# A mixture of experts on one core: tokens gathered in quarter rows and turned by VectorE instead of TensorE

## The chip, the cores and the metric

The program runs on one core of a Trainium2 chip. The metric is the device time of one execution in microseconds (us), the median over runs. PE is TensorE, DVE is VectorE, ACT is ScalarE, POOL is GpSimd; SP only issues loads and stores.

## What is computed

Two batches of 2048 tokens of 512 numbers go through cross attention, a quantised feed-forward layer, a mixing layer, and then a feed-forward layer of 16 experts. Each stage works on the layer norm of its input and adds its result to it. Only the last stage matters here:

```
logits = x @ Wg + bg                       # [2, 2048, 16]
probs  = softmax over the tokens           # each expert weighs all tokens
vals, idx = top_k(probs of one expert, 128)
tok = x[batch, idx]                        # 2 x 16 x 128 tokens of 512
h   = relu(tok @ w1[e] + b1[e])
h   = relu(h @ w2[e] + b2[e])
out = (h @ w3[e] + b3[e]) * vals
y   = zeros.at[batch, idx].add(out)
```

## The kernel before, in words

The first three stages run tile by tile (32 tiles of 128 tokens) and write the normed input of the last stage, xn4, to memory, one row of 2 KB for each token, besides the running result `out`. Then the tokens of each expert are chosen, and the experts follow. For the first four experts of batch 0 this is done early ("early experts", `early_tokens`). The rest are the twelve "joint" experts 4 to 15 for both batches (256 tokens each; e counts them from 0 to 11), and the first four experts of batch 1 alone ("single", s from 0 to 3, 128 tokens each), which are put into the joint experts e = 1, 4, 7 and 9 (`SINGLE`).

A product of a joint expert is made in three passes: each operand is split into a rounded part ("hi", made by ACT) and the rest ("lo", made by DVE: `lo`, L1973), for weights (1 MB each; `split_hi`, `split_lo`) as for tokens (`token_hi`, `token_lo`). A layer of a joint expert (`hidden`) is 48 matmuls, its last product (`outputs`) 24. Singles multiply in plain fp32.

The order on each engine is written out by hand, and each engine works through its list in order:

- PE, for each e: [`single_tokens`], `hidden(e, 0)`, [`single_first`], `tokens(e+1)`, `outputs(e-1)`, [`single_second`], `hidden(e, 1)`, [`single_outputs`]; what stands in brackets only where a single belongs to e. `tokens` turns the gathered rows of the next expert with eight transposes of 128 by 128 into PSUM, `single_tokens` those of a single with four; the products need the features on the partitions.
- DVE, for each e: `split_lo`, two `hidden_lo`, `token_lo(e+1)` out of PSUM, then twice `split_lo` and `weighted(e-1, n)`, then two `hidden_lo`.
- ACT the same in the hi parts; it also copies the turned tokens of a single (`single_copy`).
- POOL issues the indirect DMAs: `gather(e)` fetches the 128 token rows of each batch (two DMAs of 128 rows of 2 KB), `gather_single(s)` one more, `add(e)` and `add_single(s)` add results to rows of `out`. At the start of the joint experts its order is: `gather(0)`, `gather(1)`, `gather_single(0)`, `add_early(3)`, then for each e `gather(e+2)`, [`gather_single(s+1)`, `add_single(s)`,] `add(e-1)`.
- SP loads raw weights three ahead; `load_raw(i)` waits until the lo part of weight i - 3 is made.

The list of the chosen tokens comes as rows of numbers, is turned by PE and written to `ids` by DVE (semaphore k_pos = 1); the weights `vals` follow (k_pos = 2). PE runs idle products (`keep_warm`) up to the first tokens.

Of the kernel before, what the change touches and what calls it, by code (L numbers as in the profile page):

```python
# [48 lines left out]
def build(nc, io):  # L49
# [36 lines left out]
        p_ev a_ev p_sv a_sv s_gather  # L86
# [32 lines left out]
    segbase = place("segbase", [P, 1])  # L119
    bq = place("bq", [P, C])  # L120
# [167 lines left out]
    assert top[0] <= at_xt1, (top[0], at_xt1)  # L288
    tok_s = place("single_tok", [P, D], at=at_lists)
# [5 lines left out]
    tok_h, tok_l = place("tokT_h", [P, C, B * P], F32R), place("tokT_l", [P, C, B * P], F32R)  # L295
    tokT_s, h1_s = place("single_tokT", [P, D]), place("single_h1", [P, D])
# [61 lines left out]
    def four_transposes(pe, bank, src):  # L358

        for c in range(C):  # L360
            last = pe.transpose(bank[:, c * P:(c + 1) * P], src[:, c * P:(c + 1) * P], ident[:, :])  # L361
        return last

# [200 lines left out]

    def used(eng, i):
# [11 lines left out]
    def _(sp):  # L577
# [45 lines left out]
        sp.dma_start(segbase[:, :], io.segbase).then_inc(sm.c_late, 16)  # L623
        for dst, src in ((b1, io.b1), (b2, io.b2), (b3, io.b3)):
            sp.dma_start(dst[:, :], rows_on_all(src, E)).then_inc(sm.c_late, 16)
        def load_early(i):

            layer, e = ((0, 0), (0, 1), (1, 0), (1, 1), (2, 0), (2, 1),
                        (0, 2), (0, 3), (1, 2), (1, 3), (2, 2), (2, 3))[i]
            sp.dma_start(w_e[RING[i % 5]][:, :, :], chunked(io.w[layer][e])).then_inc(sem_early[i % 5], 16)  # L630
# [57 lines left out]
        def load_raw(i):  # L688
            e, layer = order[i]
            if i >= RAW:  # L690
                sp.wait_ge(sm.a_w, i - RAW + 1)
                lo_done(sp, i - RAW)
            sp.dma_start(w_raw[i % RAW][:, :, :], chunked(io.w[layer][FIRST + e])).then_inc(sem_raw[i % RAW], 16)

        def load_single(s, layer):

            i = 3 * s + layer
            if i < 4:
                sp.wait_ge(sm.p_ev, EV["y3"])
            else:  # L700
                at, was = divmod(i - 4, 3)
                sp.wait_ge(sm.p_sv, 4 * at + was + 2)
            sp.dma_start(w_e[i % 4][:, :, :], chunked(io.w[layer][s])).then_inc(sem_early[i % 4], 16)
# [39 lines left out]
    def _(pe):  # L743
# [240 lines left out]
        def early_tokens(e):  # L984

            bank = early_bank(EV[f"t{e}"] - 1)
            pe.wait_ge(sem_tok_e[e], 16)
            four_transposes(pe, bank, tok_e[e]).then_inc(sm.p_ev, 1)
# [313 lines left out]
        keep_warm(2, warm, ps_y[0])  # L1302
# [4 lines left out]
        def tokens(e):  # L1307
            for b in range(B):
                pe.wait_ge(sem_tok[e % 2][b], 16 * (e // 2 + 1))
                if e == 0:  # L1310
                    pe.wait_ge(sm.k_pos, 2)
                else:
                    pe.wait_ge(sm.d_tlo, B * (e - 1) + b + 2)
                    if b == 1 and e - 1 in SINGLE:
                        pe.wait_ge(sm.a_sv, 4 * SINGLE[e - 1] + 1)
                for c in range(C):
                    bank = token_bank(e, b, c)
                    last = pe.transpose(bank[:, c * P:(c + 1) * P], tok[e % 2][:, b, c * P:(c + 1) * P], ident[:, :])  # L1318
                last.then_inc(sm.p_tok, 1)

        def hidden(e, layer):
# [3 lines left out]
            if layer == 0:  # L1325
                pe.wait_ge(sm.d_tlo, 2 if e == 0 else B * (e + 1) + 1)
# [4 lines left out]
            for pair in range(2):  # L1331
# [3 lines left out]
                if layer == 1 and e in SINGLE:  # L1335
                    pe.wait_ge(sm.a_sv, 4 * SINGLE[e] + 2 + pair)
# [40 lines left out]
        def outputs(e):  # L1377
# [3 lines left out]
            for b in range(B):  # L1381
# [3 lines left out]
                if b == 1 and e in SINGLE:  # L1385
                    pe.wait_ge(sm.a_sv, 4 * SINGLE[e] + 4)
# [10 lines left out]
        def single_tokens(s, u):  # L1397

            pe.wait_ge(sm.s_gather, 16 * (s + 1))
            pe.wait_ge(sm.d_tlo, B * u + 3)  # L1400
            four_transposes(pe, ps_tok[1], tok_s).then_inc(sm.p_sv, 1)

        def single_first(s, u):
# [3 lines left out]
            pe.wait_ge(sm.a_sv, 4 * s + 1)  # L1407
            early_layer(ps_hid[2], w, tokT_s, range(C)).then_inc(sm.p_sv, 1)

        def single_second(s, u):  # L1410
# [3 lines left out]
            pe.wait_ge(sm.a_sv, 4 * s + 2)  # L1414
            early_layer(ps_hid[3], w, h1_s, range(C)).then_inc(sm.p_sv, 1)

        def single_outputs(s, u):
# [3 lines left out]
            pe.wait_ge(sm.a_sv, 4 * s + 3)  # L1421
# [40 lines left out]
        tokens(0)  # L1462
        keep_warm(3, wh, ps_y[0])
        for e in range(JOINT):
            if e in SINGLE:
                single_tokens(SINGLE[e], e)
# [3 lines left out]
            if e + 1 < JOINT:  # L1470
                tokens(e + 1)
# [14 lines left out]
    def _(act):  # L1486
# [413 lines left out]
        def single_copy(s):  # L1900

            act.wait_ge(sm.p_sv, 4 * s + 1)
            act.activation(tokT_s[:, :], ps_tok[1][:, :], ACT.Copy).then_inc(sm.a_sv, 1)

        def single_relu(s, layer):

            act.wait_ge(sm.p_sv, 4 * s + 2 + layer)
# [3 lines left out]
        def single_weighted(s, u):  # L1911

            act.wait_ge(sm.p_sv, 4 * s + 4)
# [6 lines left out]
        token_hi(0)  # L1920
        nxt = AHEAD
        for e in range(JOINT):
# [3 lines left out]
            if e in SINGLE:  # L1926
                single_copy(SINGLE[e])
# [6 lines left out]
            if e + 1 < JOINT:  # L1934
                token_hi(e + 1)
# [16 lines left out]
    def _(dve):  # L1952
# [571 lines left out]
        dve.tensor_scalar(top_v[:, :], ge[1][0:HEADS, :], gmax[:, 3:4], None, ALU.mult).then_inc(sm.k_out, 1)  # L2524
        dve.wait_ge(sm.k_tr, 2)
# [8 lines left out]
        def token_lo(e):  # L2534
            for b in range(B):
                t = slice(b * P, (b + 1) * P)
                for i, part in enumerate(token_parts(e, b)):
                    dve.wait_ge(sm.a_thi, B * e + b + 1 + (i if e == 0 else 1))
                    lo(sm.d_tlo, tok_l[:, part, t], in4(token_bank(e, b, part.start))[:, part, :], tok_h[:, part, t])
# [18 lines left out]
        token_lo(0)  # L2558
        split_lo(1)
        nxt = 2  # L2560
        for e in range(JOINT):
# [5 lines left out]
            if e + 1 < JOINT:  # L2567
                token_lo(e + 1)
            for n in range(2):
# [3 lines left out]
                if e >= 1:  # L2573
                    weighted(e - 1, n)
            hidden_lo(e, 1, 0)
# [12 lines left out]
    def _(pool):  # L2588
# [219 lines left out]
        def gather_single(s):  # L2808

            if s >= 1:  # L2810
                pool.wait_ge(sm.p_sv, 4 * s - 3)
            r = E + s
            pool.indirect_dma_start(
                out=tok_s[:, :], out_offset=None, in_=io.xn4,
                in_offset=bass.IndirectOffsetOnAxis(ap=ids[:, r:r + 1], axis=0),
            ).then_inc(sm.s_gather, 16)

        def add_single(s, u):

            r = E + s  # L2820
            pool.wait_ge(sm.a_sv, 4 * s + 4)
# [5 lines left out]

        def gather(e):
            if e >= 2:
                pool.wait_ge(sm.p_tok, B * (e - 1))  # L2830
            for b in range(B):
                r = b * E + FIRST + e
                pool.indirect_dma_start(
                    out=tok[e % 2][:, b, :], out_offset=None, in_=io.xn4,
                    in_offset=bass.IndirectOffsetOnAxis(ap=ids[:, r:r + 1], axis=0),
                ).then_inc(sem_tok[e % 2][b], 16)
# [19 lines left out]
        gather(0)  # L2856
# [44 lines left out]
LATE = 16 * 7  # L2901
# [36 lines left out]
```

## Time and profile before

| | |
|---|---|
| median of 3 runs | 745.3 us (744.64 to 745.97) |
| span of the profiled execution | 743.2 us, from the first to the last instruction |
| its own device time | not listed apart from the span; the median of the runs is 2.1 us above the span |
| PE busy | 716.2 us, 96% of the span |
| DVE, ACT, POOL busy | 521.6, 401.9 and 420.4 us |
| mean granted clock of PE | 0.991 |

The joint experts fill the time from 475 to 735 us of the span. A timeline's line gives the start, the duration, the engine, the line of the kernel, the operation with what it writes and reads, and in brackets how long the engine had been idle and who released it. The clock is a share of full speed, 1.00 for 2.4 GHz and 0.50 for 1.2 GHz.

### The profile page before, as it was taken

The numbers are of one execution on the slowest core, as the hardware profiler recorded it, in microseconds if no ns is written. First come the engines' busy times: TensorE is split into PE (matmuls) and PEld (weight loads), VectorE is DVE, ScalarE is ACT, GpSimd is POOL, SyncE is SP. The second block draws the span as 40 slices with busy tenths as digits, with TensorE's granted clock in tenths as the row PEclk, the third lists the DMA queues.
The fourth block names the chain that finished last, engine by engine and source line by source line (L and its number), as shares of the span: only waits on it lengthen the run. The fifth ranks groups of instructions, "written<-read, shape, count | busy, mean of one in ns | idle before, by whom it ended". The sixth has DMA issues, their size and how long they took to land.

```text
span 743.2 us, 12766 instructions
## 1 busy us (share of the span) xinstructions
PE 716.2 (96%) x4513; PEld 624.9 (84%) x4513; DVE 521.6 (70%) x978; ACT 401.9 (54%) x680; POOL 420.4 (57%) x621
## 2 busy tenths in 40 slices
PE   6999999999999999999999799999999999999994
PEld 5765888888888888888888778798999899899894
DVE  5786789889888888876896697464663565463561
ACT  5755444444544545868668334364664656464641
POOL 2825788888888887786788622503521443340132
PEclk9999999999999999999999899999999999999998
DMA  9610121221222213111117898696796698895534
GB/s 317 256 30 15 43 86 62 88 86 58 88 79 82 71 58 108 52 60 44 49 45 264 322 396 279 149 391 186 222 370 185 185 330 293 289 266 167 142 86 58
DMA packets 61671, 118.04 MB, mean 159 GB/s; under 512 B 6056, under 2 KB 7464, under 8 KB 61608
## 3 DMA queue, kind: packets, MB, share of 16 engines
q1 hardware_dynamic: 54312, 100.44, 38.7%
q0 software_dynamic: 7296, 16.78, 10.3%
q8 instruction: 37, 0.61, 0.3%
q14 instruction: 26, 0.21, 0.1%
HBM read 91.76 MB, written 25.21 MB: 157 GB/s over the span
## 4 chain that ended last, share of the span: by engine, by line
PE 84%; issue 6%; DMA 4%; DVE 3%; ACT 2%; POOL 1%; POOLq 0%; SPq 0%; DVEq 0%; ACTq 0%
PE bank L354 39%; PE banks L354 9%; PE bank L361 6%; PE bank L994 6%; PE banks L861 4%; PE banks L867 4%; DMA out<-y,ids 3%; PE banks L871 2%; PE banks L994 2%; PE banks L872 2%; PE banks L1423 1%; PE banks L1028 1%; PE bank L1318 1%; PE bank L1041 1%; DMA out<-x 1%
## 5 line engine op out<-in xcount | busy, mean ns | idle before, releaser
L2844 POOL DMA_INDIRECT out<-y,ids x24 | 46.1, 1922 | 157.4 <-DVE y L2555 155.5
L1973 DVE TENSOR_TENSOR w_l<-w_raw,w_h 128x2048 fp32r<-128x2048 f32 x35 | 80.1, 2291 | 63.2 <-ACT w_h L1496 49.4
L1961 DVE BATCH_NORM_STATS2 bn<-x 128x6 f32<-128x512 f32 x113 | 77.7, 688 | 8.2 <-DMA x<-x 5.4
L1496 ACT ACTIVATE w_h<-w_raw 128x2048 fp32r<-128x2048 f32 x36 | 68.5, 1918 | 7.2 <-DMA w_raw<-w 7.2
L1892 ACT ACTIVATE h<-bank,b 128x512 f32<-128x512 f32 x48 | 33.0, 688 | 62.5 <-PE bank L354 57.8
L1973 DVE TENSOR_TENSOR hT_l<-h,hT_h 128x512 fp32r<-128x512 f32 x48 | 33.0, 689 | 39.8 <-ACT hT_h L1898 37.7
L354 PE MATMUL bank<-tokT_h,w_h 128*128 128x256 f32 x188 | 55.1, 293 | 0.0
L2607 POOL TENSOR_SCALAR rstd<-mean_var 128x1 f32<-128x1 f32 x108 | 25.7, 238 | 50.9 <-DVE mean_var L1966 42.6
L354 PE MATMUL bank<-tokT_h,w_l 128*128 128x256 f32 x188 | 53.2, 283 | 0.0
L354 PE MATMUL bank<-tokT_l,w_h 128*128 128x256 f32 x188 | 53.2, 283 | 0.0
L354 PE MATMUL bank<-wf_h,xdT_h 128*128 128x512 f32 x128 | 52.6, 411 | 0.0
L354 PE MATMUL bank<-wf_h,xdT_l 128*128 128x512 f32 x128 | 50.3, 393 | 0.0
L354 PE MATMUL bank<-hT_h,w_h 128*128 128x256 f32 x176 | 50.1, 285 | 0.0
L354 PE MATMUL bank<-wf_l,xdT_h 128*128 128x512 f32 x128 | 50.0, 390 | 0.0
L354 PE MATMUL bank<-hT_l,w_h 128*128 128x256 f32 x176 | 49.8, 283 | 0.0
L354 PE MATMUL bank<-hT_h,w_l 128*128 128x256 f32 x176 | 49.8, 283 | 0.0
L1650 ACT ACTIVATE q<-bank,bq 128x512 f32<-128x512 f32 x32 | 22.0, 688 | 45.0 <-PE bank L354 44.5
L2687 POOL TENSOR_TENSOR x<-x,mix_bias 128x512 f32<-128x512 f32 x32 | 41.3, 1292 | 1.9 <-PE bank L361 1.8
L2625 POOL TENSOR_TENSOR qT_l<-q,qT_h 128x512 fp32r<-128x512 f32 x32 | 41.4, 1295 | 0.7 <-ACT qT_h L1652 0.7
L2723 POOL TENSOR_TENSOR x<-x,ffn_bias 128x512 f32<-128x512 f32 x32 | 41.8, 1305 | 0.0
L1492 ACT ACTIVATE xn<-x,rstd 128x512 f32<-128x512 f32 x32 | 26.1, 816 | 24.4 <-POOL rstd L2622 20.8
L1973 DVE TENSOR_TENSOR xdT_l<-bank,xdT_h 128x512 fp32r<-128x512 f32 x32 | 22.0, 689 | 23.7 <-ACT xdT_h L1496 23.4
(419 smaller groups left out, 2380.1 us busy)
## 6 DMA issues: line engine op xcount, KB each, us to landing
w_raw<-w SPq DMA_DIRECT2D x36, 1024.0 KB
early_w<-w SPq DMA_DIRECT2D x24, 1024.0 KB, 10.0
x<-x SPq DMA_DIRECT2D x32, 256.0 KB, 2.7
out<-x SPq DMA_DIRECT2D x32, 256.0 KB, 2.0
xn<-xn SPq DMA_DIRECT2D x32, 256.0 KB
mask<-mask_t SPq DMA_DIRECT2D x8, 256.0 KB, 3.4
slot_all<-slots SPq DMA_DIRECT2D x4, 512.0 KB, 7.8
stage<-wk SPq DMA_DIRECT2D x1, 1024.0 KB, 7.7
```

The lines of the kernel that those rows point to most:

```text
L354: last = pe.matmul(out, a, b, start=(n == 0), stop=(n == 3 * len(pairs) - 1))
L361: last = pe.transpose(bank[:, c * P:(c + 1) * P], src[:, c * P:(c + 1) * P], ident[:, :])
L861: last = pe.matmul(both_halves[:, a, 0:WIDE], xh[:, d, :], wc_h[:, d, a, :], start=(d == 0), stop=(d == C - 1))
L994: last = pe.matmul(bank[:, c * P:(c + 1) * P], w[:, d, c * P:(c + 1) * P], x[:, d * P:(d + 1) * P], start=(d == 0), stop=(d == C - 1))
L1496: act.activation(dst, src, ACT.Copy).then_inc(sem, 1)
L1892: act.activation(h32[n % 2][:, :], ps_hid[n % 4][:, :], ACT.Relu, bias=bias)
L1961: dve.bn_stats(bn6[which][:, j % 2, :], src[:, :]).then_inc(sem_bn[which], 1)
L1973: dve.tensor_tensor(dst, src, hi_part, ALU.subtract).then_inc(sem, 1)
L2625: pool.tensor_tensor(dst, src, hi_part, ALU.subtract).then_inc(sem, 1)
L2687: pool.tensor_tensor(x2[j % 2][:, :], x2[j % 2][:, :], cbias[:, batch(j), :], ALU.add).then_inc(sm.g_x2b, 1)
L2723: pool.tensor_tensor(x1_of(k)[:, :], x1_of(k)[:, :], fbias[:, :], ALU.add).then_inc(sm.g_x1b, 1)
L2844: pool.indirect_dma_start(out=out_rows, out_offset=bass.IndirectOffsetOnAxis(ap=ids[:, r:r + 1], axis=0), in_=y[e % 2][b][:, :], in_offset ...
```

## The change

The tokens of all joint experts but the first, and of the singles, are no longer gathered as whole rows. The row of 512 numbers is taken as four quarters of 128. One indirect DMA now fetches, for 32 tokens, the four quarters of each onto four groups of 32 partitions, so a set of 128 tokens takes four DMAs of 128 pieces of 512 bytes instead of one of 128 pieces of 2 KB. DVE then turns the 32 by 32 blocks of the result (`turn_blocks`, one instruction for 128 tokens), which puts feature 4p + c on partition p. ACT and DVE make the hi and lo parts out of that SBUF copy, for both batches in one instruction each, instead of out of PSUM in two. `tokens` and `single_tokens` leave PE, and `single_copy` leaves ACT. The first joint expert and the early experts are gathered and turned as before, but PE reads their rows with a step of four, and the weights of the first layers are loaded with four rows for each partition in one piece of 8 KB. The numbers of the quarter rows (`quarter_ids`) are made once: ACT repeats the chosen numbers times four, PE turns them with four transposes, and DVE adds the number of the quarter.

```diff
+    quarter_ids = place("quarter_ids", [P, C, ROWS], U32, at=at_seg)
+    tok_raw = place("tokT_raw", [P, C, B * P], at=at_qt + 4 * KB)
+    def of_chunk(rows, c):
+        return rows[:, c::C]
+    def turn_blocks(eng, out, rows):
+        return eng.transpose(out.rearrange("p c (t k) -> p t c k", k=QBLK),
+                             rows.rearrange("p (t k c) -> p t c k", t=P // QBLK, c=C))
+    def expert_weights(layer, e):
+        w = io.w[layer][e]
+        return w.rearrange("(p c) n -> p c n", c=C) if layer == 0 else chunked(w)
@@ @block.tensor, end of the choice @@
-        keep_warm(2, warm, ps_y[0])
+        pe.wait_ge(sm.a_rep, 1)
+        for t in range(C):
+            last = pe.transpose(ps[5][:, 2 * t * ROWS:2 * t * ROWS + HEADS], exps[0:HEADS, t * P:(t + 1) * P],
+                                ident[0:HEADS, 0:HEADS])
+        last.then_inc(sm.k_tq, 1)
@@ @block.tensor, joint experts @@
-        tokens(0)
+        first_tokens()
         for e in range(JOINT):
-            if e in SINGLE:
-                single_tokens(SINGLE[e], e)
             hidden(e, 0)
             if e in SINGLE:
                 single_first(SINGLE[e], e)
-            if e + 1 < JOINT:
-                tokens(e + 1)
@@ @block.scalar @@
+        act.wait_ge(sm.k_ids, 1)
+        act.activation(exps[0:HEADS, :].rearrange("p (t q k) -> p t q k", t=C, k=QBLK),
+                       top_i[:, :].rearrange("p (t k) -> p t k", k=QBLK).unsqueeze(2)
+                       .to_broadcast([HEADS, C, P // QBLK, QBLK]), ACT.Copy, scale=float(P // QBLK)).then_inc(sm.a_rep, 1)
...
         def token_hi(e):
-            for b in range(B):
-                act.wait_ge(sm.p_tok, B * e + b + 1)
-                act.wait_ge(sm.p_h, max(0, 4 * (e - 1) + 2))
-                for part in token_parts(e, b):
-                    hi(sm.a_thi, tok_h[:, part, b * P:(b + 1) * P], in4(token_bank(e, b, part.start))[:, part, :])
+            act.wait_ge(sm.d_tr, B * e)
+            hi(sm.a_thi, tok_h[:, :, :], tok_raw[:, :, :])
...
             for n in range(2):
                 if nxt < len(order) and (e > 0 or n == 1):
                     split_hi(nxt)
                     nxt += 1
+                if n == 0 and e + 1 < JOINT:
+                    token_hi(e + 1)
@@ @block.vector @@
+        dve.wait_ge(sm.k_tq, 1)
+        dve.tensor_scalar(quarter_ids[:, :, :],
+                          ps[5][:, 0:2 * C * ROWS].rearrange("p (t r) -> p t r", t=C)[:, :, 0:HEADS:2],
+                          quarter[:, 0:1], None, ALU.add).then_inc(sm.k_quart, 1)
         dve.wait_ge(sm.k_tr, 2)
         dve.tensor_copy(vals[:, :], ps[0][:, 0:HEADS:2]).then_inc(sm.k_pos, 1)
...
+        def turn_tokens(e):
+            dve.wait_ge(sm.p_h, 4 * e - 2)
+            for b in range(B):
+                dve.wait_ge(sem_tok[e % 2][b], tokens_in(e))
+                turn_blocks(dve, tok_raw[:, :, b * P:(b + 1) * P], tok[e % 2][:, b, :]).then_inc(sm.d_tr, 1)
+        def token_lo(e):
+            dve.wait_ge(sm.a_thi, e + 3)
+            lo(sm.d_tlo, tok_l[:, :, :], tok_raw[:, :, :], tok_h[:, :, :])
+        def turn_single(s):
+            dve.wait_ge(sm.s_gather, 64 * (s + 1))
+            if s >= 1:
+                dve.wait_ge(sm.p_sv, 3 * s - 2)
+            turn_blocks(dve, tokT_s[:, :].rearrange("p (c t) -> p c t", c=C), tok_s[:, :]).then_inc(sm.d_ts, 1)
...
             hidden_lo(e, 0, 0)
             hidden_lo(e, 0, 1)
             if e + 1 < JOINT:
-                token_lo(e + 1)
+                turn_tokens(e + 1)
+            if e + 1 in SINGLE:
+                turn_single(SINGLE[e + 1])
             for n in range(2):
                 if nxt < len(order):
                     split_lo(nxt)
                     nxt += 1
                 if e >= 1:
                     weighted(e - 1, n)
+                if n == 0 and e + 1 < JOINT:
+                    token_lo(e + 1)
@@ @block.gpsimd @@
+        xn4_quarters = io.xn4.rearrange("n (q f) -> (n q) f", q=P // QBLK)
         def gather(e):
-            if e >= 2:
-                pool.wait_ge(sm.p_tok, B * (e - 1))
+            if e == 2:
+                pool.wait_ge(sm.p_tok, B)
+            if e >= 3:
+                pool.wait_ge(sm.d_tr, B * (e - 2))
             for b in range(B):
                 r = b * E + FIRST + e
-                pool.indirect_dma_start(
-                    out=tok[e % 2][:, b, :], out_offset=None, in_=io.xn4,
-                    in_offset=bass.IndirectOffsetOnAxis(ap=ids[:, r:r + 1], axis=0),
-                ).then_inc(sem_tok[e % 2][b], 16)
+                for t in range(C):
+                    pool.indirect_dma_start(
+                        out=tok[e % 2][:, b, t * P:(t + 1) * P], out_offset=None, in_=xn4_quarters,
+                        in_offset=bass.IndirectOffsetOnAxis(ap=quarter_ids[:, t, r:r + 1], axis=0),
+                    ).then_inc(sem_tok[e % 2][b], 16)
...
         pool.wait_ge(sm.k_pos, 1)
-        gather(0)
+        first_gather()
+        pool.wait_ge(sm.k_quart, 1)
         gather(1)
         gather_single(0)
         add_early(3)
```

## Rows read from the trace of the kernel before

**Rows 1.** Busy time by engine, joint experts (us, busy (instructions) PE PEld DVE ACT POOL, clock, DMA share, GB/s).

```profile
475.00:735.00 260.00, 258.75 (x1844) 239.22 (x1844) 142.71 (x131) 140.85 (x167) 82.15 (x53) 1.00 0.76 231
```

**Rows 2.** The chain that ended last, in order of time (start us, us, what).

```profile
487.75 0.44 PE bank L361 x4
488.19 5.76 PE bank L354 x48
493.95 3.57 PE bank L994 x32
497.52 0.87 PE bank L1318 x8
498.40 5.47 PE banks L354 x24
...
646.28 5.75 PE bank L354 x48
...
664.55 5.76 PE bank L354 x48
```

**Rows 3.** GpSimd's timeline (start us, us, line, operation, idle before and releaser).

```profile
468.60 1.03 POOL L2833 DMA_INDIRECT tok<-xn,ids  x1 [3.62 <-DMA out<-early_tok,early_ids]
469.93 0.98 POOL L2833 DMA_INDIRECT tok<-xn,ids  x1 [0.30 <-issue]
471.22 0.95 POOL L2833 DMA_INDIRECT tok<-xn,ids  x1 [0.31 <-issue]
472.47 0.94 POOL L2833 DMA_INDIRECT tok<-xn,ids  x1 [0.30 <-issue]
...
556.26 2.52 POOL L2833 DMA_INDIRECT tok<-xn,ids  x1 [0.30 <-issue]
...
642.78 1.76 POOL L2844 DMA_INDIRECT out<-y,ids  x1 [7.33 <-DVE y L2555]
644.85 1.02 POOL L2833 DMA_INDIRECT tok<-xn,ids  x1 [0.30 <-issue]
```

**Rows 4.** GpSimd's timeline at the early experts: last logit gather, its first reader.

```profile
426.24 0.94 POOL L2778 DMA_INDIRECT early_logit<-cut,early_logit_ids  x1 [0.30 <-issue]
432.35 0.20 POOL L2789 TENSOR_TENSOR early_shift<-early_logit,cut_tops 128x4 f32<-128x4 f32 x1 [5.17 <-DMA early_logit<-cut,early_logit_ids]
```

**Rows 5.** TensorE's timeline: after the long wait; first reader of the second gather.

```profile
417.79 1.11 PE L915 MATMUL bank<-ident,lg_wide 128*128 128x128 f32 x4 [4.95 <-DVE lg_wide L2124]
...
473.44 0.44 PE L1318 MATMUL bank<-ident,tok 128*128 128x128 f32 x2 [0.27 <-issue]
```

**Rows 6.** VectorE's timeline.

```profile
475.22 2.28 DVE L1973 TENSOR_TENSOR w_l<-w_raw,w_h 128x2048 fp32r<-128x2048 f32 x1
...
482.44 0.69 DVE L1973 TENSOR_TENSOR hT_l<-h,hT_h 128x512 fp32r<-128x512 f32 x1 [2.13 <-ACT hT_h L1898]
...
555.64 2.29 DVE L1973 TENSOR_TENSOR w_l<-w_raw,w_h 128x2048 fp32r<-128x2048 f32 x1 [1.11 <-ACT w_h L1496]
...
641.70 0.81 DVE L2555 TENSOR_SCALAR y<-banks,b,vals 128x512 f32<-128x512 f32 x1
```

**Rows 7.** Busy time by engine in short stretches (columns as in rows 1).

```profile
416.00:418.00 2.00, 0.21 (x1) 0.22 (x2) 1.49 (x7) 2.00 (x3) 1.24 (x4) 0.51 0.75 290
422.00:423.00 1.00, 1.00 (x7) 1.00 (x7) 1.00 (x5) 0.00 (x0) 0.55 (x1) 0.57 0.99 377
424.00:430.00 6.00, 6.00 (x56) 6.00 (x56) 5.90 (x16) 1.27 (x3) 2.57 (x3) 1.00 1.04 398
486.00:490.00 4.00, 4.00 (x36) 4.00 (x35) 3.93 (x4) 3.16 (x5) 0.00 (x0) 1.00 1.03 401
655.00:660.00 5.00, 5.00 (x31) 4.42 (x30) 4.11 (x4) 2.91 (x2) 0.56 (x1) 1.00 0.99 296
```

**Rows 8.** ScalarE's timeline: the last exponential of the token choice.

```profile
466.89 0.40 ACT L1876 ACTIVATE ge<-top_v,gmax 63x128 f32<-63x128 f32 x1 [0.33 <-DVE gmax L2510]
```

**Rows 9.** The load queue's timeline: three 1 MB loads.

```profile
478.02 4.25 SPq L703 DMA_DIRECT2D early_w<-w  x3
```

More of the change, by code:

```diff
@@ L119, in build @@
     segbase = place("segbase", [P, 1])
+    quarter = place("quarter", [P, 1])
     bq = place("bq", [P, C])
@@ L362, in four_transposes, with four_row_transposes @@
         return last
+    def of_chunk(rows, c):
+        return rows[:, c::C]
+    def four_row_transposes(pe, bank, rows):
+        for c in range(C):
+            last = pe.transpose(bank[:, c * P:(c + 1) * P], of_chunk(rows, c), ident[:, :])
+        return last
+    def turn_blocks(eng, out, rows):
[4 more added lines that the diff above has]
+        return w.rearrange("(p c) n -> p c n", c=C) if layer == 0 else chunked(w)
     def blocks(t):
@@ L563, in token_bank, with tokens_in @@
         return ps_y[1] if (e, b) == (0, 1) and c >= 2 else ps_tok[b]
+    def tokens_in(e):
+        return 64 * (e // 2) + (16 if e % 2 == 0 else 64)
     def used(eng, i):
@@ L623, in _ @@
         sp.dma_start(segbase[:, :], io.segbase).then_inc(sm.c_late, 16)
+        sp.dma_start(quarter[:, :], io.quarter).then_inc(sm.c_late, 16)
         for dst, src in ((b1, io.b1), (b2, io.b2), (b3, io.b3)):
@@ L1301, in _, with first_tokens @@
         pe.transpose(ps[1][:, 0:HEADS], top_i[:, :], ident[0:HEADS, 0:HEADS]).then_inc(sm.k_tr, 1)
-        keep_warm(2, warm, ps_y[0])
+        pe.wait_ge(sm.a_rep, 1)
[3 more added lines that the diff above has]
+        last.then_inc(sm.k_tq, 1)
         pe.wait_ge(sm.k_out, 1)
         pe.transpose(ps[0][:, 0:HEADS], top_v[:, :], ident[0:HEADS, 0:HEADS]).then_inc(sm.k_tr, 1)
-        def tokens(e):
+        def first_tokens():
             for b in range(B):
[L1309 to L1315, printed above, removed]
+                pe.wait_ge(sem_tok[0][b], 16)
+                pe.wait_ge(sm.k_pos, 2)
                 for c in range(C):
-                    bank = token_bank(e, b, c)
-                    last = pe.transpose(bank[:, c * P:(c + 1) * P], tok[e % 2][:, b, c * P:(c + 1) * P], ident[:, :])
+                    bank = token_bank(0, b, c)
+                    last = pe.transpose(bank[:, c * P:(c + 1) * P], of_chunk(tok[0][:, b, :], c), ident[:, :])
                 last.then_inc(sm.p_tok, 1)
@@ L1325, in hidden @@
             if layer == 0:
-                pe.wait_ge(sm.d_tlo, 2 if e == 0 else B * (e + 1) + 1)
+                pe.wait_ge(sm.d_tlo, 2 if e == 0 else e + 3)
                 xh, xl = tok_h, tok_l
@@ L2532, in split_lo, with first_token_lo @@
             lo(sm.d_w, w_l[i % WR][:, :, :], w_raw[i % RAW][:, :, :], w_h[i % WR][:, :, :])
-        def token_lo(e):
+        def first_token_lo():
             for b in range(B):
                 t = slice(b * P, (b + 1) * P)
-                for i, part in enumerate(token_parts(e, b)):
-                    dve.wait_ge(sm.a_thi, B * e + b + 1 + (i if e == 0 else 1))
-                    lo(sm.d_tlo, tok_l[:, part, t], in4(token_bank(e, b, part.start))[:, part, :], tok_h[:, part, t])
+                for i, part in enumerate(token_parts(0, b)):
+                    dve.wait_ge(sm.a_thi, b + 1 + i)
+                    lo(sm.d_tlo, tok_l[:, part, t], in4(token_bank(0, b, part.start))[:, part, :], tok_h[:, part, t])
+        def turn_tokens(e):
+            dve.wait_ge(sm.p_h, 4 * e - 2)
+            for b in range(B):
+                dve.wait_ge(sem_tok[e % 2][b], tokens_in(e))
[8 more added lines that the diff above has]
+            turn_blocks(dve, tokT_s[:, :].rearrange("p (c t) -> p c t", c=C), tok_s[:, :]).then_inc(sm.d_ts, 1)
         def hidden_lo(e, layer, pair):
@@ L2556, in weighted @@
                               ALU.add, ALU.mult).then_inc(sm.d_y, 1)
-        token_lo(0)
+        first_token_lo()
         split_lo(1)
@@ L2925 @@
     arrays["later"] = -(p[:, None] > p[None, :]).astype(np.float32)
+    arrays["quarter"] = (p // 32).astype(np.float32).reshape(P, 1)
     arrays["segbase"] = (p // 64 * 2048 + p % 4 * 512).astype(np.float32).reshape(P, 1)
```

65 lines of the change are left out of this document (33 added, 32 removed).

## The prediction

> **What bounds the kernel now.** I read the busy time of the joint experts first. Of 260 us between 475 and 735, PE is busy 258.75 at full clock, DVE 142.71, ACT 140.85, POOL 82.15 [rows 1]. The reader is to see that this stage ends when PE ends, and that whatever leaves PE's list is a gain as long as nothing on PE begins to wait. The chain of waits in order of time says the same piece by piece: a layer of 48 matmuls takes 5.75 us, an output of 24 takes 5.47, a single's layer 3.57, the eight transposes of an expert 0.87, the four of a single 0.44, one behind the other without a gap [rows 2]. Then POOL's timeline, because gathers are multiplied by four there; DVE's, which gets a new place to wait; the short stretches for the clock and the DMA share.
>
> **What leaves PE.** Eleven expert turns of 0.87 and four single turns of 0.44: 9.57 + 1.76 = 11.33 us [rows 2]. This is all that can be won here. ACT's single copies and the PSUM reads of ACT and DVE are off the path (both are idle over 40% of the stage [rows 1]).
>
> **What POOL gets.** Gathers follow each other every 1.25 us (471.22, then 472.47), of which 0.94 to 1.03 is the DMA instruction itself [rows 3]. Does a gather of 64 KB cost less to issue than one of 256 KB? The logit gathers fetch 128 pieces of 4 bytes and take 0.94 us [rows 4], so the price goes with the 128 indices, not the bytes. I take 1.25 each. Gathers grow by 6 for each of 11 experts and by 3 for each of 4 singles: 78 more, 97.5 us; POOL's 82 of 260 become 180. That fits on average. It doesn't fit where a gather has no lead, and there are two such places, both singles, because `turn_single` now waits on DVE one expert earlier, in front of the `split_lo` and `token_lo` that the next first layer on PE needs.
>
> **First place: expert 1.** Its single 0 is gathered twelfth after `gather(0)`. The first quarter gather starts at 471.22, where `gather(1)` starts now [rows 3]; the new list isn't later (ACT's copy of 63x512, between 0.40 for 63x128 and DVE's 0.69 for 128x512, four small transposes and one DVE operation come after ACT's last exponential, over at 467.29, and shortly before `gather(0)` at 468.60; they are done near 470 [rows 3, 6, 8]). The twelfth starts at 471.22 + 11 x 1.25 = 484.97 and ends at 485.9. One hit comes on top: a gather that starts while DVE subtracts weights (2.29 us) is held to about 0.85 us past that operation's end (started 556.26, lasted 2.52 instead of 0.98; DVE's began at 555.64 [rows 3, 6]). DVE subtracts from 475.22 to 477.50, so some 1.2 us: 487.1.
>
> Landing: `gather(0)`'s second DMA left POOL at 470.91 and PE reads it at 473.44, 2.5 us at most [rows 3, 5]. The last logit gather left at 427.18 and its reader came at 432.35, 5.2 us, with the DMA engines full (share 1.04) [rows 4, 7]. At 486 to 490 the share is 1.03 now [rows 7], but the next load hangs on the delayed `split_lo`, so the three megabytes issued from 478.02 on [rows 9] will be nearly through; I take 4.0 and keep 2.5 and 5.2. So 491.1. The Trainium skill, "DMA: Bandwidth & Descriptors", section "Anatomy of one DMA — SWDGE (gpsimd) path", gives some 2.0 us plus bytes over 436 GB/s, an estimate of 2.15 us here; by it the two places together would cost 3.7 us less, and the logit row speaks against it where the engines are full.
>
> Then on DVE: the turn, `split_lo` 2.29, `token_lo` for 128x1024 at half of that, 1.15, handovers 0.2. No DVE turn is in the trace. The nearest row is a subtraction of 128x512 out of SBUF, 0.69 us [rows 6], which I take; the upper bound is a 128x2048 operation, 2.29 (each number at four times the price), the lower 0.6. The Trainium skill, "SBUF — State Buffer", section "Door 1: The DMA port swizzle", in its note on 16-byte lines, says that an access that goes to a new line each time pays a penalty; the turn reads with a step of four numbers, 16 bytes. No row here shows such a step, so the sum stays with 0.69; by the page it would move to the upper bound, some 3 us more in all.
>
> 491.1 + 0.69 + 2.29 + 1.15 + 0.2 = 495.4, where PE starts this layer at 487.95 now (488.19 in the chain, which models ends [rows 2]): 7.5 later. The bounds are 492.6 (+4.7: no hit, landing 2.5) and 499.4 (+11.5: two hits, 5.2, slow turn). PE is done with expert 0 at about 487.6 and idles for some 8 us; its eight transposes there covered a handover, so their removal brings nothing forward.
>
> The clock: after 4.95 us of idling [rows 5] PE ran at a granted 0.50, the 1.2 GHz level, from about 417.8 until 422.9 [rows 7]; 5.1 us at half speed lose 2.5. I add 2.5 here (bounds 0 and 2.5): 10.0 in all.
>
> What else queues there is covered: `add_early(3)`, behind the twelve gathers, lets `relu(0,1,0)` go near 493 instead of 485, and `gather(2)` lands near 506, but expert 1 holds a single, and its 27 us on PE (two layers, an output and three single products of some 3.6) give DVE and ACT the time.
>
> **Second place: expert 9.** Count from T, the start of expert 8's first layer, 646.28 now [rows 2]. `gather(10)` follows the second `add(6)`, whose y DVE ends at 642.51; that is tied to PE by the single of expert 7 and stays. So it starts no earlier than T - 1.4 [rows 3], and single 3 comes behind its eight DMAs: the twelfth ends at T - 1.4 + 11 x 1.25 + 0.95 = T + 13.3. One hit, 1.2, and POOL's own lag: between `gather(2)` at 489 and this point lie 84 gathers and 16 adds (105 + 28 us) and up to 21 hits (25 us) in some 158 us, so POOL is about full and 0 to 4 us behind; I take 1.5. T + 16.0, landed T + 20.0; turn 0.69, `split_lo` 2.29, `weighted` 0.81 [rows 6], `token_lo` 1.15, 0.2: T + 25.2. PE starts expert 9 at T + 18.3 now [rows 2]: 6.9 later, and 2.5 of clock (it idles from T + 17.0), 9.4. Bounds: T + 20.8, that is +2.5 without the clock, and T + 29.4, +11.1 with it 13.6.
>
> **Where nothing waits.** Singles 1 and 2 are gathered one round of POOL earlier; by the same count single 1 lands some 2 us before its turn, single 2 hardly before, with 1 us left at expert 7. Expert turns have a round of lead. In an expert without a single `token_lo` ends some 3.5 us before PE needs it, which covers two turns even at 2 us. `quarter_ids` puts k_pos = 2 back by 0.5, of which 0.2 shows, as PE waits for the gather anyway. The strided PE reads of six token sets are bounded by nothing and doubling (6 x 0.4, not all on the path); I take 0. The 8 KB weight pieces gain nothing, since no PE wait is put down to a load.
>
> **Sum.** Transposes not eaten by the two places: 11.33 - 2 x (0.87 + 0.44) = 8.7 won. 10.0 + 9.4 + 0.2 - 8.7 = 10.9 us longer: span 754, and as the median stands 2.1 above the span, 756 us. All lower bounds: 4.7 + 2.5 - 8.7 = -1.5, 744. All upper: 14.0 + 13.6 + 0.2 - 8.7 and up to 2 of strided reads, 766.
>
> **Rivals.**
> 1. It is hidden: the singles land before DVE wants them, and only the transposes go. 11.33 less about 0.8 of the handover they covered: 735. It decides from a last single gather landed by 483.6 (487.95 - 4.35), so issue below (483.6 - 2.5 - 471.2) / 12 = 0.83 us each. For it: POOL is idle for two thirds of the stage [rows 1]. Against it: 1.25 us apart, and 0.94 for 4-byte pieces [rows 3, 4].
> 2. The waits come at their lowest price, the gathers landing in 2.5 us without a hit, and idling of 4 to 5 us leaves the clock alone: 744, even or a hair faster. For it: the loads are held back too, so the DMA engines may be free. Against it: the one row with 4.95 us idle lost the clock.
> 3. POOL becomes the bound: hits pile up, it falls over 4 us behind, expert 7 waits too, adds come late: 766. For it: 133 us of issue in 158. Against it: during each DVE wait no weight is subtracted, so there are no hits.
>
> **Chances.** Forecast 0.62 (its own range 748 to 763), rival 1 0.07, rival 2 0.15, rival 3 0.16. The predicted time is 756. For 8 in 10 the range must reach into rivals 2 and 3: 744 to 766. A change below 0.2% is about what a measurement of this kernel can't tell from none. Faster: rival 1 and a part of 2, 0.13; same: most of the rest of 2, 0.10; slower 0.77.
>
> **What the new profile would show.** Quarter gathers 1.25 us apart, twelve of them after 471; POOL busy near 180 us in the stage; DVE turns near 0.7 us; PE idle before the first layers of experts 1 and 9, released by DVE's `token_lo` (L1973), with the clock at 0.5 behind both; no gap elsewhere above 1 us; transposes gone from the chain. I'd be wrong if quarter gathers were issued in under 0.85 us, if they landed at once, if a turn took several us (then every expert waits), or if the idle PE kept its clock.

## The result and the profile after

The changed kernel takes 763.6 us (median of 4 runs, 759.76 to 764.61) against 745.2 us before: ratio 1.024, 95% interval 1.021 to 1.027. It is slower, as forecast, by 18.4 us where 10.9 were expected. The profiled execution is the quickest of the four (759.76, span 757.9); the others ran at a lower mean granted clock (0.972 to 0.976 for 0.980), and where their 3 to 5 us more went isn't shown. Here is its stage of the joint experts, and four short stretches of it (columns as in rows 1):

```profile
475.00:750.00 275.00, 252.14 (x1725) 231.65 (x1724) 164.72 (x145) 139.89 (x152) 186.10 (x129) 0.96 0.74 218
486.00:489.00 3.00, 3.00 (x16) 3.00 (x16) 1.65 (x2) 1.32 (x2) 2.54 (x4) 0.54 1.04 365
496.00:499.00 3.00, 3.00 (x16) 3.00 (x16) 2.24 (x4) 2.52 (x3) 2.39 (x3) 0.50 0.87 281
622.00:624.00 2.00, 1.65 (x8) 1.68 (x9) 2.00 (x2) 0.36 (x1) 1.70 (x2) 0.50 0.93 385
680.00:682.00 2.00, 1.98 (x9) 2.00 (x10) 2.00 (x2) 0.00 (x0) 1.22 (x1) 0.50 0.98 414
```

PE was busy all but 1.25 of 260 us before [rows 1]; now it idles for 22.9 of 275, and four times it runs at the 1.2 GHz level. GpSimd went from 82 to 186 us. What PE waited for in this stage (who for whom, us in total, times, longest):

```profile
PE bank L357 <- ACT w_h L1513: 11.4, 1, 11.4
PE bank L357 <- DVE tokT_l L1991: 5.6, 2, 3.1
PE bank L1390 <- issue: 4.0, 1, 4.0
PE bank L1390 <- DVE hT_l L1991: 1.1, 1, 1.1
```

The 11.4 is put down to a weight's hi part that was long done; on VectorE's timeline below `token_lo` ends at 679.77, and PE starts at 680.02. The 2.55 and 3.09 stand before experts 1 and 7. The ledger: 22.1 us of waits, 5.6 of half clock (59 products spaced about 0.215 us instead of 0.120 in the four stretches), less the 11.33 of transposes, makes 16.4. PE's timeline, before and then after, has the first product of the stage and that of expert 1, and after the change that of expert 9:

```profile
475.12 0.35 PE L1345 MATMUL bank<-tokT_h,w_h 128*128 128x256 f32 x1 [0.32 <-DVE tokT_l L1973]
...
487.95 0.36 PE L354 MATMUL bank<-tokT_h,w_h 128*128 128x256 f32 x1
```

```profile
472.96 0.36 PE L1372 MATMUL bank<-tokT_h,w_h 128*128 128x256 f32 x1 [0.40 <-DVE tokT_l L1991]
...
494.18 0.36 PE L357 MATMUL bank<-tokT_h,w_h 128*128 128x256 f32 x1 [2.55 <-DVE tokT_l L1991]
...
680.02 0.55 PE L357 MATMUL bank<-tokT_h,w_h 128*128 128x256 f32 x1 [11.42 <-ACT w_h L1513]
```

From the stage's first product to the end the kernel took 268.07 us before (475.12 to 743.19) and 284.98 now (472.96 to 757.94): 16.9. The stage itself began 2.2 earlier in this execution; over the fourteen profiles of this study that start lies anywhere between 472.96 and 476.76, so it is not the change's.

GpSimd's timeline after (columns as in rows 3): the first single's last gather, two held gathers, the third single's last, then the run before expert 9. A gather is called held where its instruction takes much longer than the usual 0.95 us.

```profile
483.97 0.95 POOL L2859 DMA_INDIRECT single_tok<-xn,quarter_ids  x1 [0.30 <-issue]
...
493.91 3.03 POOL L2892 DMA_INDIRECT tok<-xn,quarter_ids  x1 [0.30 <-issue]
497.25 0.95 POOL L2892 DMA_INDIRECT tok<-xn,quarter_ids  x1 [0.30 <-issue]
498.50 2.70 POOL L2892 DMA_INDIRECT tok<-xn,quarter_ids  x1 [0.30 <-issue]
...
611.39 0.94 POOL L2859 DMA_INDIRECT single_tok<-xn,quarter_ids  x1 [0.30 <-issue]
...
658.32 1.02 POOL L2892 DMA_INDIRECT tok<-xn,quarter_ids  x1 [0.30 <-issue]
...
672.18 0.95 POOL L2859 DMA_INDIRECT single_tok<-xn,quarter_ids  x1 [0.30 <-issue]
```

VectorE's timeline after, before experts 1, 7 and 9:

```profile
489.48 1.13 DVE L379 STREAM_TRANSPOSE single_tokT<-single_tok 128x512 f32<-128x512 f32 x1 [1.83 <-DMA single_tok<-xn,quarter_ids]
490.53 2.25 DVE L1991 TENSOR_TENSOR w_l<-w_raw,w_h 128x2048 fp32r<-128x2048 f32 x1
492.70 1.22 DVE L1991 TENSOR_TENSOR tokT_l<-tokT_raw,tokT_h 128x1024 fp32r<-128x1024 f32 x1
493.84 2.29 DVE L1991 TENSOR_TENSOR w_l<-w_raw,w_h 128x2048 fp32r<-128x2048 f32 x1
...
498.09 2.29 DVE L1991 TENSOR_TENSOR w_l<-w_raw,w_h 128x2048 fp32r<-128x2048 f32 x1 [0.76 <-ACT w_h L1513]
...
616.93 1.14 DVE L379 STREAM_TRANSPOSE single_tokT<-single_tok 128x512 f32<-128x512 f32 x1 [4.74 <-DMA single_tok<-xn,quarter_ids]
...
620.16 0.80 DVE L2596 TENSOR_SCALAR y<-banks,b,vals 128x512 f32<-128x512 f32 x1
...
674.66 1.08 DVE L379 STREAM_TRANSPOSE single_tokT<-single_tok 128x512 f32<-128x512 f32 x1 [13.24 <-DMA single_tok<-xn,quarter_ids]
675.66 2.25 DVE L1991 TENSOR_TENSOR w_l<-w_raw,w_h 128x2048 fp32r<-128x2048 f32 x1
677.83 0.81 DVE L2596 TENSOR_SCALAR y<-banks,b,vals 128x512 f32<-128x512 f32 x1
678.55 1.22 DVE L1991 TENSOR_TENSOR tokT_l<-tokT_raw,tokT_h 128x1024 fp32r<-128x1024 f32 x1
```

Each time VectorE stands idle until a single's quarters have landed, then turns them, and only then makes what PE is waiting for. The two held gathers overlap weight subtractions (493.84 and 498.09).

The 4.0 and 1.1 us at expert 0 look like a loss of their own, but they cost nothing: expert 1's first layer starts 21.22 us after the stage's first product here, and 21.30 in two runs below whose traces have no such gap. They only moved a part of the wait before expert 1 forward. Why ACT's `relu` of expert 0 came late there is open.

### The profile page after: what moved, and what is told of

Same layout as the page of the kernel before. It is cut to its first block, busy times and chain, and to the rows that moved or that the text cites. A ratio compares the mean times of both kernels' runs of the same rounds, so it can differ in the third digit from the quotient of the medians.

```text
span 757.9 us, 12607 instructions
## 1 busy us (share of the span) xinstructions
PE 711.2 (94%) x4411; PEld 619.8 (82%) x4411; DVE 546.6 (72%) x994; ACT 401.8 (53%) x666; POOL 527.3 (70%) x699
## 4 chain that ended last, share of the span: by engine, by line
PE 63%; POOL 11%; issue 8%; DMA 6%; DVE 5%; ACT 3%; another core or an unknown queue 1%; POOLq 0%; SPq 0%; DVEq 0%; ACTq 0%
PE bank L357 29%; POOL tok L2892 6%; PE bank L364 5%; PE bank L1022 5%; PE banks L357 5%; PE banks L889 4%; PE banks L895 3%; DMA out<-y,ids 2%; POOL single_tok L2859 2%; PE banks L1022 2%; POOL out L2903 2%; PE banks L899 2%; PE banks L900 2%; DMA single_tok<-xn,quarter_ids 1%
## 5 line engine op out<-in xcount | busy, mean ns | idle before, releaser
L2892 POOL DMA_INDIRECT tok<-xn,quarter_ids x88 | 114.2, 1297 | 26.7 <-issue 26.7
L357 PE MATMUL bank<-tokT_h,w_h 128*128 128x256 f32 x188 | 57.1, 304 | 17.1 <-ACT w_h L1513 11.4
L357 PE MATMUL bank<-tokT_l,w_h 128*128 128x256 f32 x188 | 55.1, 293 | 0.0
L357 PE MATMUL bank<-tokT_h,w_l 128*128 128x256 f32 x188 | 55.1, 293 | 0.0
L357 PEld LDWEIGHTS bank<-tokT_h,w_h 128*128 128x128 f32 x188 | 38.2, 203 | 18.5 <-ACT w_h L1513 11.6
L1667 ACT ACTIVATE q<-bank,bq 128x512 f32<-128x512 f32 x32 | 22.1, 690 | 44.8 <-PE bank L357 44.4
## 6 DMA issues: line engine op xcount, KB each, us to landing
early_w<-w SPq DMA_DIRECT2D x24, 1024.0 KB, 11.4
```

The lines of the kernel that those rows point to most:

```text
L357: last = pe.matmul(out, a, b, start=(n == 0), stop=(n == 3 * len(pairs) - 1))
L2892: pool.indirect_dma_start(out=tok[e % 2][:, b, t * P:(t + 1) * P], out_offset=None, in_=xn4_quarters, in_offset=bass.IndirectOffsetOnAxis( ...
```

## The experiments

Theory A: the cost is VectorE waiting for a single's late quarters in front of work that PE needs, and the half clock behind. Theory B: VectorE's turning time. Theory C: GpSimd can't issue the gathers in time. Theory D: the layout. Stage length means from the stage's first product to the end: 268.07 before, 284.98 after.

**The single's turn at its own expert.** In VectorE's loop:

```diff
-            if e + 1 in SINGLE:
-                turn_single(SINGLE[e + 1])       # behind turn_tokens(e + 1)
+            if e in SINGLE:
+                turn_single(SINGLE[e])           # first in the expert's list
```

> Each single's turn moved on VectorE from the expert before it to the start of its own expert, behind that expert's token remainders; nothing else. Theory A (the cost is VectorE waiting for a single's late quarter gathers in front of work that TensorE needs, and the half clock after each such wait): the waits of 2.55, 3.09 and 11.42 us before experts 1, 7 and 9 and some 4.5 us of half clock go, 763.6 - 21.5 = 742, range 738 to 748. Theory B (VectorE's turning time itself): the turns are all still there, 758 to 764. Theory C (GpSimd can't issue the gathers fast enough, whoever waits for them): the joint experts' own gathers are late next, 750 to 758.

Measured 757.5 us (ratio 1.015, 1.013 to 1.018), in C's range. The wait before expert 7 is gone; the other two are not. What PE waited for:

```profile
PE bank L1022 <- DVE single_tokT L379: 8.9, 2, 8.7
PE banks L1444 <- issue: 3.4, 2, 1.7
PE bank L357 <- DVE tokT_l L1991: 3.3, 1, 3.3
```

The 8.7 is single 3's own first layer: its gathers stand behind the eight of `gather(10)`, as GpSimd's timeline shows, and are over at 680.4.

```profile
674.51 0.94 POOL L2892 DMA_INDIRECT tok<-xn,quarter_ids  x1 [0.30 <-issue]
675.76 0.94 POOL L2859 DMA_INDIRECT single_tok<-xn,quarter_ids  x1 [0.30 <-issue]
...
679.50 0.94 POOL L2859 DMA_INDIRECT single_tok<-xn,quarter_ids  x1 [0.30 <-issue]
```

The 3.3 before expert 1 are its own tokens (first layer 15.95 us after the stage's start, 12.83 before): eight quarter gathers in place of two land too late without any single in front. A alone falls.

**Singles in whole rows, turned by TensorE.**

```diff
-            for t in range(C):
-                pool.indirect_dma_start(
-                    out=tok_s[:, t * P:(t + 1) * P], out_offset=None, in_=xn4_quarters,
-                    in_offset=bass.IndirectOffsetOnAxis(ap=quarter_ids[:, t, r:r + 1], axis=0),
+            pool.indirect_dma_start(
+                out=tok_s[:, :], out_offset=None, in_=io.xn4,
+                in_offset=bass.IndirectOffsetOnAxis(ap=ids[:, r:r + 1], axis=0),
...
+            if e in SINGLE:
+                single_tokens(SINGLE[e], e)      # PE; ACT copies the bank, VectorE turns no single
             hidden(e, 0)
```

> The singles go back to one gather of whole rows and TensorE's turn (four transposes of 0.44 us in all, each single); the joint experts stay in quarter rows. GpSimd issues 12 gathers fewer (15 us), VectorE turns no single. A: the waits at experts 1, 7 and 9 go, TensorE pays 4 x 0.44 = 1.8 us: 738 to 748, near the first run. B: only four turns of 1.1 us less, 757 to 762. C: 12 of 92 gathers less, 748 to 757.

Measured 751.9 us (1.010, 1.007 to 1.013): in C's range again, above A's. PE still waited 5.7 us for a single, the fourth, though it is one gather now:

```profile
PE bank L374 <- DMA single_tok<-xn,ids: 6.9, 2, 5.7
PE bank L357 <- DVE tokT_l L2006: 1.5, 1, 1.5
```

**The layout alone.** The kernel before with `expert_weights` and the step-of-four reads:

```diff
-                    last = pe.transpose(bank[:, c * P:(c + 1) * P], tok[e % 2][:, b, c * P:(c + 1) * P], ident[:, :])
+                    last = pe.transpose(bank[:, c * P:(c + 1) * P], of_chunk(tok[e % 2][:, b, :], c), ident[:, :])
```

> The kernel before with the new order of the features alone: first-layer weights in pieces of 8 KB a partition, TensorE's transposes read with a step of four. No quarter gathers, no turning by VectorE. A: strided reads cost nothing, the weights gain nothing: 744 to 746. Theory D (the 8 KB pieces bring the joint experts' start forward by the 2.2 us seen after the change): 742 to 743.5. If the strided reads cost time, over 747.

Measured 745.8 us (1.0005, 0.9995 to 1.0015): no change in the whole. The 8 KB pieces gain nothing, and D falls: the stage began at 475.07. The strided reads do cost a little, as one expert's eight transposes show, first in the kernel before and then here:

```profile
497.36 1.04 PE L1318 MATMUL bank<-ident,tok 128*128 128x128 f32 x8
```

```profile
497.44 1.13 PE L1333 MATMUL bank<-ident,tok 128*128 128x128 f32 x8
```

Over eleven experts that is 1.0 us, and the stage is 1.0 us longer (269.08 for 268.07), too little for the whole time to show.

**Every joint turn twice.**

```diff
+                then(turn_blocks(dve, tok_raw[:, :, b * P:(b + 1) * P], tok[e % 2][:, b, :]))
                 turn_blocks(dve, tok_raw[:, :, b * P:(b + 1) * P], tok[e % 2][:, b, :]).then_inc(sm.d_tr, 1)
```

> Each turn of a joint expert's tokens is done twice by VectorE (22 more turns of 1.05 us, 23 us in all); the singles' turns are as after the change. A: where a single is late VectorE has time to spare, elsewhere it has some 100 us of idle time in the stage: 763 to 768. B: near the full 23 us, 775 to 787.

Measured 767.9 us (1.031, 1.030 to 1.033). The group of the turns (nanoseconds least/median/most):

```profile
L379 DVE STREAM_TRANSPOSE tokT_raw<-tok x44: 1040/1102/1132, 484.6 to 727.7; 128x512 f32<-128x512 f32 x44
```

22 more turns of 1.10 us, 24 us, cost 4.3, in A's range: B falls. VectorE has the time wherever it isn't made to wait.

**The single's gathers first on GpSimd**, with the turn where the change put it:

```diff
         for e in range(JOINT):
+            if e - 1 in SINGLE and SINGLE[e - 1] + 1 < FIRST:
+                gather_single(SINGLE[e - 1] + 1)
             if e + 2 < JOINT:
                 gather(e + 2)
             if e >= 1:
                 if e - 1 in SINGLE:
-                    if SINGLE[e - 1] + 1 < FIRST:
-                        gather_single(SINGLE[e - 1] + 1)
                     add_single(SINGLE[e - 1], e - 1)
```

> The changed kernel with one thing moved on GpSimd: at experts 2, 5 and 8 the next single's four gathers stand ahead of the eight of the joint expert after next, not behind them; the turn of the single stays where the change put it. They start some 10 us earlier, so the waits of 3.09 and 11.42 us before experts 7 and 9 and the 2.9 us of half clock after them should go, 763.6 - 17.4 = 746, and what is late at expert 1 stays. If GpSimd's order is the cause of the late singles: 745 to 750. If the joint experts' gathers, now 5 us later, become the next wait: 752 to 758. If the place of the turn on VectorE is all that counts: no change, 760 to 764.

Measured 758.9 us (1.019, 1.017 to 1.022): a miss, outside all three ranges. At experts 1 and 9 VectorE still gets to the single's turn before the quarters land. At expert 7 it is now the joint expert's own second half that is late, and PE waits 4.1 us there instead of 3.09: theory C, at one place. VectorE's timeline at experts 1, 7 and 9:

```profile
491.36 1.08 DVE L379 STREAM_TRANSPOSE single_tokT<-single_tok 128x512 f32<-128x512 f32 x1 [4.20 <-DMA single_tok<-xn,quarter_ids]
...
619.90 1.13 DVE L379 STREAM_TRANSPOSE tokT_raw<-tok 128x512 f32<-128x512 f32 x1 [4.33 <-DMA tok<-xn,quarter_ids]
...
672.94 1.09 DVE L379 STREAM_TRANSPOSE single_tokT<-single_tok 128x512 f32<-128x512 f32 x1 [6.51 <-DMA single_tok<-xn,quarter_ids]
```

**Both, order and place.** The two diffs together.

> The same order on GpSimd, and the single's turn at the start of its own expert as in the first run (757.5). There 8.66 us before the fourth single's first layer and some 1.6 us of half clock were left: 757.5 - 10.3 = 747, range 745 to 750 if GpSimd's order is the cause; 753 to 758 if the joint experts' gathers are late in its place.

Measured 745.7 us (1.0005, 0.998 to 1.003), in the first range and level with the kernel before. Order alone brought 4.7 us, place alone 6.2, both 17.9: each leaves the other's wait standing. So the loss has two parts that only show together: GpSimd's queue makes the quarters late, and VectorE's list makes others wait for them.

**Singles in whole rows, and first.**

> The same order on GpSimd with the singles in whole rows turned by TensorE as in the second run (751.9). There TensorE waited 5.66 us for the fourth single and lost some 1.2 us at half clock around it: 751.9 - 6.9 = 745, range 743 to 747 if GpSimd's order is the cause; 750 to 752 if not.

Measured 740.4 us (0.994, 0.992 to 0.996): faster than before, and 2.6 us under the expected range, which was worked out from the four scattered times of the second run (748.9 to 755.1). The 5.7 us wait is down to 0.7; left is 2.2 us before expert 1.

**The second joint expert in whole rows too.** `tokens(1)`, `token_hi(1)` and `token_lo(1)` are as in the kernel before, and

```diff
         last.then_inc(sm.k_tq, 1)
+        keep_warm(2, warm, ps_y[0])
         pe.wait_ge(sm.k_out, 1)
...
-        first_gather()
-        pool.wait_ge(sm.k_quart, 1)
-        gather(1)
+        first_gather(0)
+        first_gather(1)                          # two DMAs of whole rows
         gather_single(0)
```

> The run before this one, and the second joint expert too is gathered in whole rows and turned by TensorE (0.87 us), so that GpSimd has 6 gathers fewer before expert 1; and two more 512-column products keep TensorE at work while the quarter numbers are made. If what was late at expert 1 (1.28 and 1.49 us of waits, some 1.6 us at half clock) is due to the gathers issued there one after another, and the half clock before the joint experts' stage (1.0 us) to TensorE's pause: 745 - 4.4 - 1.0 + 0.9 = 740.5, range 738 to 743, under the kernel before. If GpSimd's issue is not what is late there: 744 to 747.

Measured 735.4 us (0.989, 0.985 to 0.992), again 2.6 us under the range. Against the run before this one the stage is 5.1 us shorter (258.29 for 263.38) and starts 1.4 us earlier. The idle products can only have brought the second, and that start varies by more among the profiles. The same 260 us of it as in rows 1:

```profile
475.00:735.00 260.00, 248.98 (x1752) 229.19 (x1751) 159.13 (x140) 141.26 (x157) 174.32 (x112) 0.99 0.78 231
```

No wait of PE is left in the stage but 0.7 us at its start, and the clock doesn't fall in it while PE has work. Ten expert turns of 0.87 are off PE: 745.1 - 8.7 = 736.4. GpSimd is still busy for 174 us, and VectorE turns 20 sets. So neither is too much in itself.

**Idle products ahead of the late experts.** To price the half clock, on the changed kernel:

```diff
             if layer == 0:
+                keep_warm({1: 30, 7: 12, 9: 45}.get(e, 0), wh, ps_tok[0])
                 pe.wait_ge(sm.d_tlo, 2 if e == 0 else e + 3)
```

> The changed kernel with products whose result nobody reads (512 columns, 0.213 us each at 2.4 GHz) ahead of the waits for the tokens' remainders: 30 at expert 1, 12 at expert 7, 45 at expert 9. They take no wait away; if the half clock that follows each wait is a cost of its own (1.6, 1.4 and 1.5 us, counted from the spacing of the products after the three waits), 763.6 - 4.5 = 759, range 757 to 761. If the half clock comes whatever TensorE does there, 763 to 765.

Measured 779.8 us (1.048, 1.045 to 1.050): a miss, and a lesson on the wait. The products stood behind `weights(i)`, and PE's timeline shows them starting when it was nearly over:

```profile
494.65 8.58 PE L775 MATMUL bank<-w_h 128*128 128x512 f32 x30 [7.53 <-DVE w_l L1992]
```

So PE waits for the weights' lo part first, which stands behind the single's turn as `token_lo` does, and the products added their own length.

**Singles in quarter rows in the best kernel**, with order and place right.

> The best kernel so far (735.4) with the singles in quarter rows again, turned by VectorE at the start of their own expert and gathered ahead of the joint expert after next. TensorE is rid of 4 x 0.44 = 1.8 us, GpSimd has 12 gathers more. If VectorE and GpSimd have room for the singles once place and order are right: 733.5 to 735. If 12 gathers of 1.25 us still push others back (waits of 1.70 us for the single's last layer and 2.10 us at expert 7 were left in the run that had place and order right): 737 to 742.

Measured 739.5 us (0.994, 0.991 to 0.996), in the second range and some 4.7 us more than the best kernel on the same chip: PE waited 3.4 us before expert 7, whose own quarters came late, and GpSimd had 185 us to do instead of 177. Not all of the 4.7 need be the singles': in the two profiled executions the stage is 3.1 us longer, and it starts 2.5 us later, behind a stretch of half clock (469.9 to 473.3) that the best kernel's doesn't have. Even so the singles' 1.76 us on PE are not worth twelve gathers.

**The best kernel again.**

> The same kernel as the best one (second joint expert and singles in whole rows, the singles' gathers ahead, two more products), timed in more rounds: 733 to 738, ratio to before 0.985 to 0.992.

Measured 734.9 us (0.987, 0.985 to 0.989), as expected. It is faster than both kernels, 1.3% below the one before.

**Idle work that depends on nothing.**

```diff
             i = when[(e, layer)]
+            for _ in range({1: 60, 7: 28, 9: 95}.get(e, 0) if layer == 0 else 0):
+                pe.transpose(ps_tok[0][:, 0:P], ident[:, :], ident[:, :])
             wh, wl = weights(i)
```

> The changed kernel with idle work that depends on nothing: transposes of the identity into a bank that nobody reads (0.109 us each, from 0.87 us for eight), 60 ahead of expert 1's first layer, 28 ahead of expert 7's and 95 ahead of expert 9's, now ahead of the wait for the weights' remainder too (the products of the run before the last stood behind it, began only when it was over, and so added their own length). They fill 6.5, 3.1 and 10.4 us of the three waits. If the half clock after the waits costs what the spacing of the products says, 763.6 - 4.5 = 759, range 757 to 761; if it costs nothing there, 762 to 765.

Measured 767.0 us (1.029, 1.027 to 1.032), above both ranges. The 95 ran on to 689.3 with pauses of their own, while `token_lo` of expert 9 was done at 683.9, and the clock still fell to 0.50 at experts 1 and 9. At expert 7 it stayed up, and there the run does tell something: from expert 7's first layer to expert 8's it takes 28.74 us, as much as the changed kernel's 28.72 with its half clock. An undisturbed expert with a single, expert 4 of the changed kernel, takes 27.33. What PE no longer loses to the clock it now waits for the single's last product:

```profile
650.03 0.67 PE L1446 MATMUL banks<-early_w,single_h 128*128 128x512 f32 x1 [1.25 <-issue]
```

So the spacing of the products says what the half clock takes from PE, not what a kept clock would give back. At expert 7 that was nothing; at the other places no run shows it.

## Why the prediction was right, and where it was short

- **What leaves PE**: right. Ten expert turns of 0.87 are 8.7 us, and from expert 1's first layer to expert 11's the best kernel takes 8.65 us less than the one before (214.22 for 222.87). Its whole stage is 9.8 shorter; the rest lies outside the turns (1.7 behind expert 11's start, less 0.6 lost at expert 1).
- **What GpSimd gets**: right. Quarter gathers follow every 1.25 us (481.47, 482.72, 483.97), so the price goes with the 128 indices. That 186 us in the stage came so near to the forecast 180 is luck: the 97.5 counts the 0.30 between two issues, which busy time doesn't (78 times 0.95 is 74), and some 30 us of holds made that up.
- **Expert 1**: right in place, price and mechanism, not whole. Expert 1 starts 8.4 us later after the stage's first product (21.22 for 12.83), where 7.5 was worked out. The last gather left POOL at 484.92, which is 11.96 after that product; 487.1, or 11.98, was forecast. The quarters took 4.6 us (to 489.48; 4.0 taken), the turn 1.13 (0.69 taken), `token_lo` 1.22 (1.15). What I hadn't seen: 3.1 of the 8.4 would be there without the single, from expert 1's own eight gathers.
- **Expert 9**: right in place and mechanism, too small. The step that failed is GpSimd's lag, "I take 1.5". With T = 651.63, `gather(10)` started at 658.32, T + 6.7, where T - 1.4 was free of lag: 8.1 us. The twelve ended at T + 21.5 without a hit, landed 1.5 us later, and PE started at T + 28.4, not T + 25.2. So the lag was 6.6 us too small, and it was luck that only 3.2 of it showed: no gather was held here (1.2), and the landing was 2.5 shorter than taken. The count behind the 1.5 was wrong in three terms. From `gather(2)` up to `gather(10)` there are 72 gathers, not 84; the other twelve are counted again behind T - 1.4, which is 15 us too many. The holds, put at up to 25 us, were 32.6 over those 72. And waits of GpSimd itself were put at nothing, where it stood for 13.6 us in three places:

```profile
520.14 1.75 POOL L2903 DMA_INDIRECT out<-y,ids  x1 [3.36 <-DVE y L2596]
...
552.70 2.28 POOL L2903 DMA_INDIRECT out<-y,ids  x1 [5.19 <-DMA out<-single_y,ids]
...
621.18 2.34 POOL L2903 DMA_INDIRECT out<-y,ids  x1 [5.06 <-DVE y L2596]
```

  The last of these closes a ring: GpSimd is late with a single, VectorE waits for that single before expert 7 (616.93) and makes y behind it (620.16), and GpSimd waits for y. The page's group of quarter gathers has the holds over the whole stage (busy, mean ns):

```profile
L2892 POOL DMA_INDIRECT tok<-xn,quarter_ids x88 | 114.2, 1297 | 26.7 <-issue 26.7
```

  88 times 347 ns over the 0.95 of an unheld one is 30 us, in gathers such as the two shown, held while VectorE subtracts.
- **Expert 7**: wrong. "1 us left" to spare was 3.09 us of wait and 1.4 of half clock: the last gather left at 612.33 and the turn started at 616.93, 4.6 us later.
- **The clock**: right that it falls, the size too large: 1.2 to 1.6 us a place for 2.5, but at four stretches instead of two. That all of it is a cost of its own is not shown, and at expert 7 the last run speaks against it.
- **Landing**: 4.6, 4.6 and 1.5 us, all inside the bounds of 2.5 and 5.2 but the last. The Trainium skill, "DMA: Bandwidth & Descriptors", section "Anatomy of one DMA — SWDGE (gpsimd) path", would give an estimate of 2.15. The trace comes near it at expert 9 alone (1.5 from the issue's end, 2.5 from its start), where the DMA engines were nearly idle (share 0.23 from 668 to 672).
- **The turn**: 1.04 to 1.14 us, 1.6 times the subtraction of the same shape and half of the upper bound. Whether the 16-byte step that the Trainium skill, "SBUF — State Buffer", section "Door 1: The DMA port swizzle", warns of is the reason, no run here tells. That section gives the penalty no size, so "to the upper bound" was a guess, and it came out at half of it.
- **The strided reads of PE**, taken as 0: 0.09 us for eight transposes, so nearly right.
- **The rivals**: the 763.6 lies 0.6 above the forecast's own range of 748 to 763. Rival 1 needed gathers under 0.83 us, and they take 1.25. What came is the forecast's mechanism with half of rival 3 on top (GpSimd more than 4 us behind, expert 7 waiting too, but with its 3.09 us alone); the time lies nearer to rival 3's 766 than to 756. Rival 3's own claim, that GpSimd is the bound, is only half true: with the order changed and fewer gathers in two places it is as busy and nobody waits.

## What to carry to other kernels

An instruction on a busy engine that waits for a transfer delays all that is queued behind it, so put it as late in that engine's list as its reader allows, and put the transfer ahead of those with a longer lead; here neither alone brought half of what both did. When a change multiplies the issues of one queue, count the queue's lag at the places with the least lead, holds included, not its mean load. A part of a change can pay where it has lead and cost where it has none: ten of twelve experts gained, the four singles and the second expert lost it.

## What the runs showed of the hardware

- An indirect gather of 128 pieces costs GpSimd 0.94 to 1.03 us to issue whether a piece has 4 bytes [rows 4], 512 or 2048 [rows 3], and up to 3.75 us (at 598.40 after the change) when VectorE subtracts meanwhile. Of the 106 gathers from 466 us on, 29 took over 1.15 us, and each of them began beside a subtraction of VectorE; of the 50 that began beside none, 11 of them beside a turn, none did.
- VectorE's turn of 128x512 numbers of fp32 in blocks of 32 by 32, read with a step of four, takes 1.04 to 1.14 us.
- TensorE's fp32 transposes of 128 by 128, read with a step of four numbers, take 1.13 us for eight instead of 1.04.
- PE's granted clock fell to the 1.2 GHz level after waits of 2.55 and 3.09 us, less than the 4.95 seen before [rows 5].
